# Causal linear attention in a fused Perceiver layer: the numerator matmuls go from 64x64 to 128x64 tiles, masking is done in two halves, and the Wo split moves from steps 2, 4, 6, 8 to steps 11 to 14

## The chip, the cores and the metric

The kernel runs on one core of a Trainium2 chip. The metric is device time of one launch in microseconds (us). The engines are called PE (TensorE, matmul), PEld (its weight loads), DVE (VectorE), ACT (ScalarE), POOL (GpSimd) and SP (SyncE, which here only issues DMAs). They run in parallel, each through its own list of instructions, and meet through semaphores.

## The reference, cut to what matters

```python
x = x + cross_attention(layernorm(x), ctx, ctx, Wq, bq, Wk, bk, Wv, bv)   # x (32, 32, 256), ctx (32, 257, 256)
x = x + linear_attention(layernorm(x), Wq, Wk, Wv, Wo, W_feat)
x = x + ffn(layernorm(x), w1, w2)     # two layers, 256 -> 1024 -> 256, ternary weights, 8-bit activations, gelu between

# linear_attention: H = 16 heads of 64, 128 features; T = 32 tokens in each of 32 sequences
q, k, v = heads(x @ Wq), heads(x @ Wk), heads(x @ Wv)
phi(u)  = exp(u @ W_feat - 0.5 * sum(u * u)) / sqrt(128)
num_t   = phi(q_t) @ sum_{s<=t} outer(phi(k_s), v_s)
den_t   = phi(q_t) @ sum_{s<=t} phi(k_s) + 1e-6
y = concat_heads(num / den) @ Wo
```

## The kernel before

The 1024 tokens lie in NG = 8 groups of 128 tokens (4 sequences each). The first stage is the cross attention. It goes over the groups and ends, for the matmul engine, at about 88 us. The third stage, the output projection with Wo and the feed-forward net, goes over the groups again and takes the time from about 214 us to the end. Between them stands the loop that the change touches.

**The head loop.** It has STEPS = 16 steps s. Step s treats two heads (`pair = s // 2`, inner index a) on one half of the tokens (`h = s % 2`, four groups g of 128 tokens). Each step has these parts:

- `project(s)`: q and k of the pair, 12 matmuls of 128x128 weights on 512 columns (L991 to L993, in split precision hi and lo).
- `squares(s)` on ACT and `copies(s)` on DVE take them out of PSUM; `squares_low(s)` on POOL makes the low part of the squares (`sq_lo`, L373).
- `exponents(s, t)`: 10 matmuls with weights of 64 rows and 128 columns (L1195); `features(s)` on ACT takes the exponential (`phi`, L563).
- `attention(s)`: scores phi(k) phi(q), in blocks of PT = 64 tokens (two sequences): 32 matmuls of tile 128x64 (all 128 rows of the array, 64 of its columns), L1208. A block b of 64 keys goes to partitions 64b to 64b + 63 of PSUM bank `b45[:, h]`.
- `masked(s)` on DVE: the scores times the causal mask, into SBUF tile `smk[h]` (L861).
- `numerators(s)`: the masked scores as weights, the values `va` (64 columns and a column of ones, which gives the denominator) as the moving side: 32 matmuls on 65 columns (L1220), into PSUM `b67`. Then `outputs(s)` on DVE divides (L871, L873, L876) and writes `y`.

PE's order is written by hand: in loop index i it does `project(i)`, `exponents(i-1, 0)`, `attention(i-2)`, `numerators(i-3)`, `exponents(i-1, 1)`. For i = 3 to 15 the numerators stand right behind the attention. After the loop come `exponents(15, 0)`, `attention(14)`, `numerators(13)`, `exponents(15, 1)`, `numerators(14)`, `attention(15)`, two groups of transposes `yTt(0, .)` (L1252), `numerators(15)`, and then `yTt(1, 0)` and `project_out(0)`. On DVE the end of the loop is `masked(14)`, `outputs(13)`, `outputs(14)`, `masked(15)`, `yTc(0, 0)`, `yTc(0, 1)`, `outputs(15)`. `numerators(s)` waits for `masked(s)` and for `outputs(s-1)`; `yTt(0, .)` waits for `outputs(14)`.

**POOL's side work.** Between the squares POOL splits the weights of the next head pair (`split_pair`, L348 and L350, in odd steps up to 13; `project` of the next even step waits for it), quantises the weights of the net (`quantise_w`, L383 to L387, a piece in each even step from 4 and two at the end) and splits Wo (`split_wo`, L393 and L395, in steps 2, 4, 6, 8).

**Loads.** SP issues all large loads in a written order. W1, W2 and Wo follow one another after the last `av_cp` of the cross attention (L293 to L295), then the loop's weights of pair 1. ACT sums the absolute values of W1 in index 1 and of W2 in index 2 of its loop (`weight_sum`, L497).

Of the kernel before, what the change touches and what calls it, by code (L numbers as in the profile page):

```python
# [16 lines left out]
F32 = mybir.dt.float32  # L17
F32R = mybir.dt.float32r
# [5 lines left out]
P = 128  # L24
# [4 lines left out]
PT = 2 * T  # L29
# [17 lines left out]
def build(nc, x, ctx, ctxT, xWq, bq, xWk, bk, xWvT, bv, aWq, aWk, aWv, aWo, Wf, w1T, w2T,  # L47
          ident_d, mask_d, seq_d, out):
    with ExitStack() as stack:
        def sem(name):  # L50
            return stack.enter_context(nc.semaphore(name))
# [69 lines left out]
        sq_lo = [[z2.take(f"sq_lo{h}{t}", [P, TOK], F32R) for t in range(2)] for h in range(2)]  # L121
        sq = [[z2.take(f"sq{h}{t}", [P, TOK]) for t in range(2)] for h in range(2)]
        w1_raw = z2.take("w1_raw", [P, DC, HID])
        w2_raw = z2.take("w2_raw", [P, HC, D])
        smk = [z2.take(f"smk{h}", [P, 2 * HALF, PT]) for h in range(2)]
        z = Region(work_at)
# [14 lines left out]
        cl = z.take("cl", [P, NG, D])  # L141
        z.at = max(z.at, z2.at - 2 * size[F32] * 2 * HALF * PT)
        xn2 = [z.take(f"xn2_{i}", [P, D]) for i in range(2)]
        z.at = max(z.at, z2.at)
        xwv_hi = z.take("xwv_hi", [P, DC, D], F32R)
# [3 lines left out]
        avT_lo = z.take("avT_lo", [P, DC, P], F32R)  # L149
        wo_lo = Region(z2.at).take("wo_lo", [P, HC, D], F32R)  # L150
        z3 = Region(work_at)
# [74 lines left out]
        f_mm, f_exp = sem("f_mm"), sem("f_exp")  # L226
        s_mm, s_mask = sem("s_mm"), sem("s_mask")
        n_mm, n_den, n_rden, n_y = (sem(n) for n in ("n_mm", "n_den", "n_rden", "n_y"))
# [12 lines left out]
        def _(sp):  # L241
# [50 lines left out]
            sp.wait_ge(av_cp, NG)  # L292
            sp.dma_start(w1_raw[:], w1T.rearrange("(c p) n -> p c n", p=P)).then_inc(ld_w1, 16)  # L293
            sp.dma_start(w2_raw[:], w2T.rearrange("(c p) n -> p c n", p=P)).then_inc(ld_w2, 16)
            sp.dma_start(wo[:], aWo.rearrange("(c p) n -> p c n", p=P)).then_inc(ld_wo, 16)  # L295
            for p in range(1, PAIRS):
                sp.wait_ge(w_split, p * 4)
                load_pair(p)
# [9 lines left out]
        def _(pool):  # L308
# [80 lines left out]
            def split_wo(k):  # L389
                if k == 0:  # L390
                    pool.wait_ge(ld_wo, 16)
                at = slice(2 * k, 2 * k + 2)
                nc.gpsimd.tensor_copy(wo_hi[:, at], wo[:, at]).then_inc(wo_split, 1)  # L393
                pool.wait_ge(wo_split, 2 * k + 1)
                nc.gpsimd.tensor_tensor(wo_lo[:, at], wo[:, at], wo_hi[:, at].bitcast(F32),  # L395
                                        ALU.subtract).then_inc(wo_split, 1)

            for s in range(STEPS):
                if s % 2 == 1 and s // 2 + 1 < PAIRS:
                    split_pair(s // 2 + 1, 2 * s + 1)  # L400
                squares_low(s)
                if s in (2, 4, 6, 8):
                    split_wo(s // 2 - 1)
                if s % 2 == 0 and s >= 4:
                    quantise_w(s // 2 - 2)
# [36 lines left out]
        def _(act):  # L442
# [186 lines left out]
            yTc(0, 1)  # L629
            act.wait_ge(s_mask, STEPS)  # L630
            for i in range(NG + 1):
# [19 lines left out]
        def _(dve):  # L651
# [205 lines left out]
            def masked(s):  # L857
                dve.wait_ge(s_mm, s + 1)
                if s >= 2:
                    dve.wait_ge(n_mm, s - 1)  # L860
                nc.vector.tensor_tensor(  # L861
                    smk[s % 2][:], b45[:, s % 2, :].rearrange("p (g n) -> p g n", n=PT),
                    mask[:].rearrange("p (a n) -> p a n", a=1).broadcast_to([P, 2 * HALF, PT]),
                    ALU.mult).then_inc(s_mask, 1)

# [15 lines left out]
            for i in range(1, STEPS):  # L881
                copies(i)
                if i == 4:
                    weight_scales()
                if i >= 2:
                    masked(i - 2)
                if i >= 3:
                    outputs(i - 3)
# [99 lines left out]
        def _(pe):  # L988
# [210 lines left out]
            def attention(s):  # L1199
                h = s % 2  # L1200
                pe.wait_ge(f_exp, 4 * s + 4)
                if s >= 2:
                    pe.wait_ge(s_mask, s - 1)
                for a in range(2):
# [7 lines left out]
            def numerators(s):  # L1212
                h, pair = s % 2, s // 2
                pe.wait_ge(s_mask, s + 1)
                if s >= 1:
                    pe.wait_ge(n_y, 2 * s)
                for g in range(HALF):
                    for b, a in ((0, 0), (1, 1), (0, 1), (1, 0)):
                        keys = slice(PT * b, PT * (b + 1))
                        mm = pe.matmul(b67[keys, a, g * VW:(g + 1) * VW], smk[h][keys, a * HALF + g, :],  # L1220
                                       va[keys, HALF * h + g, pair * 2 + a, :], start=True, stop=True)
                mm.then_inc(n_mm, 1)
# [6 lines left out]
            for i in range(2, STEPS):  # L1229
# [4 lines left out]
                if i == 4:  # L1234
                    pe.wait_ge(w_sum, 2)
                    pe.wait_ge(s_mask, 2)
                    pe.matmul(b5[:, 508:510], ones[:], wsum[:, 0:2], start=True, stop=True).then_inc(w_bc, 1)
# [167 lines left out]
```

## Time and profile before

| | |
|---|---|
| median of 3 runs | 272.37 us (271.4 to 272.67) |
| the profiled execution | 272.51 us |
| its span, from the first to the last instruction | 270.4 us |
| PE busy | 252.8 us, 94% of the span |
| DVE, ACT, POOL busy | 166.4, 142.4, 134.2 us |
| mean granted TensorE clock | 0.987 of full |

The first 2.11 us of difference between time and span lie outside of the recorded instructions. A busy share says how long an engine had an instruction in flight, not that it was at its peak: records of matmuls overlap, and short pauses between the starts of two matmuls are hidden in them. So the starts of neighbouring matmuls tell more than the busy time.

### The profile page before, as it was taken

The numbers are of one execution on the slowest core, as the hardware profiler recorded it, in microseconds if no ns is written. First come the engines' busy times: TensorE is split into PE (matmuls) and PEld (weight loads), VectorE is DVE, ScalarE is ACT, GpSimd is POOL, SyncE is SP. The second block draws the span as 40 slices with busy tenths as digits, with TensorE's granted clock in tenths as the row PEclk, the third lists the DMA queues.
The fourth block names the chain that finished last, engine by engine and source line by source line (L and its number), as shares of the span: only waits on it lengthen the run. The fifth ranks groups of instructions, "written<-read, shape, count | busy, mean of one in ns | idle before, by whom it ended". The sixth has DMA issues, their size and how long they took to land.

```text
span 270.4 us, 6580 instructions
## 1 busy us (share of the span) xinstructions
PE 252.8 (94%) x2568; PEld 198.9 (74%) x2574; DVE 166.4 (62%) x424; ACT 142.4 (53%) x267; POOL 134.2 (50%) x163
## 2 busy tenths in 40 slices
PE   8878849999999999999999999999998989999975
PEld 7765628786677667777777777777776978898754
DVE  3476856766644354655566555556662669898975
ACT  0432252544435688655545565545553537877762
POOL 2331202133103478497987979495889023434430
PEclk9999977999999999999999999999999999999999
DMA  6999999991078011001010010100000000010001
GB/s 207 367 385 367 374 320 342 364 394 44 1 236 270 0 41 40 2 0 41 2 40 2 2 42 0 41 2 0 2 0 2 2 2 0 6 36 25 19 19 58
DMA packets 18541, 27.74 MB, mean 103 GB/s; under 512 B 1488, under 2 KB 11856, under 8 KB 18512
## 3 DMA queue, kind: packets, MB, share of 16 engines
q1 hardware_dynamic: 17072, 26.35, 28.5%
q10 hardware_dynamic: 1440, 0.99, 1.2%
q8 instruction: 20, 0.33, 0.5%
q14 instruction: 9, 0.07, 0.1%
HBM read 26.28 MB, written 1.05 MB: 101 GB/s over the span
## 4 chain that ended last, share of the span: by engine, by line
PE 77%; SPq 6%; DMA 6%; ACT 4%; DVE 3%; issue 3%; POOL 0%; ACTq 0%
PE b L1195 16%; PE b L991 13%; PE b L993 11%; PE b L992 11%; PE b L1220 6%; DMA wv_raw<-in_aWv 6%; PE b L1208 6%; PE b L1252 2%; SPq L273 2%; PE b L1299 2%; PE b L1340 2%; PE b L1084 2%; PE b L1063 1%; SPq L269 1%; SPq L175 1%
## 5 line engine op out<-in xcount | busy, mean ns | idle before, releaser
L563 ACT ACTIVATE phi<-b 128x512 f32<-128x512 f32 x64 | 34.8, 598 | 40.8 <-PE b L1195 40.8
L373 POOL TENSOR_TENSOR sq_lo<-sq,sq_hi 128x512 fp32r<-128x512 f32 x32 | 40.9, 1290 | 23.6 <-ACT sq_hi L506 23.0
L791 DVE CAST x_hi<-b 128x512 fp32r<-128x512 f32 x32 | 22.1, 691 | 48.7 <-ACT sq_hi L506 48.7
L325 POOL TENSOR_TENSOR lnr<-lnv,mh 128x1 f32<-128x1 f32 x16 | 8.8, 548 | 54.3 <-DVE lnv L675 54.3
L991 PE MATMUL b<-nT_lo,wp_hi 128*128 128x512 f32 x64 | 26.8, 418 | 0.0
L505 ACT ACTIVATE sq<-b 128x512 f32<-128x512 f32 x32 | 19.2, 601 | 11.8 <-PE b L993 11.8
L993 PE MATMUL b<-nT_hi,wp_hi 128*128 128x512 f32 x64 | 25.1, 393 | 0.0
L992 PE MATMUL b<-nT_hi,wp_lo 128*128 128x512 f32 x64 | 24.9, 389 | 0.0
L793 DVE TENSOR_TENSOR x_lo<-b,x_hi 128x512 fp32r<-128x512 f32 x32 | 22.1, 691 | 1.1
L1208 PEld LDWEIGHTS b<-phi,phi 128*64 128x64 f32 x512 | 16.2, 138 | 5.7 <-issue 5.5
L506 ACT ACTIVATE sq_hi<-b 128x512 fp32r<-128x512 f32 x32 | 19.1, 595 | 0.0
L991 PE MATMUL b<-wo_lo,yT_hi 128*128 128x256 f32 x64 | 18.7, 293 | 0.0
L1208 PE MATMUL b<-phi,phi 128*64 128x64 f32 x512 | 18.4, 225 | 0.0
L1220 PE MATMUL b<-va,smk 64*64 64x65 f32 x512 | 18.4, 221 | 0.0
L993 PE MATMUL b<-wo_hi,yT_hi 128*128 128x256 f32 x64 | 18.1, 282 | 0.0
L992 PE MATMUL b<-wo_hi,yT_lo 128*128 128x256 f32 x64 | 18.0, 280 | 0.0
L1195 PE MATMUL b<-x_hi,feat_hi 64*128 64x512 f32 x64 | 16.7, 492 | 1.0 <-ACT phi L563 1.0
L991 PEld LDWEIGHTS b<-nT_lo,wp_hi 128*128 128x128 f32 x64 | 12.0, 187 | 7.5 <-issue 5.1
L1220 PEld LDWEIGHTS b<-va,smk 64*64 64x64 f32 x512 | 16.2, 134 | 1.6 <-issue 0.6
L444 ACT ACTIVATE va<-b 128x512 f32<-128x512 f32 x16 | 9.6, 599 | 11.3 <-PE b L993 11.3
L680 DVE TENSOR_SCALAR xn<-res,lnm,lnr 128x256 f32<-128x256 f32 x24 | 9.8, 421 | 8.6 <-POOL lnr L325 7.3
L991 PE MATMUL b<-wv_lo,nT_hi 128*128 128x512 f32 x32 | 14.1, 442 | 0.1
(162 smaller groups left out, 646.6 us busy)
## 6 DMA issues: line engine op xcount, KB each, us to landing
cT<-in_ctxT SPq DMA_DIRECT2D x8, 1028.0 KB, 13.9
cn<-in_ctx SPq DMA_DIRECT2D x8, 1024.0 KB, 15.4
wv_raw<-in_aWv SPq DMA_DIRECT2D x1, 1024.0 KB, 15.7
wp_raw<-in_aWq SPq DMA_DIRECT2D x8, 128.0 KB, 2.2
wp_raw<-in_aWk SPq DMA_DIRECT2D x8, 128.0 KB, 2.3
w_raw<-in_w1T SPq DMA_DIRECT2D x1, 1024.0 KB, 5.1
w_raw<-in_w2T SPq DMA_DIRECT2D x1, 1024.0 KB, 7.7
wo<-in_aWo SPq DMA_DIRECT2D x1, 1024.0 KB, 11.3
```

The source lines that it names most:

```text
L373: nc.gpsimd.tensor_tensor(sq_lo[s % 2][t][:], sq[s % 2][t][:], sq_hi[s % 2][t][:].bitcast(F32), ALU.subtract).then_inc(sq_l, 1)
L505: nc.scalar.activation(sq[s % 2][t][:], proj_bank(s, t), ACT.Square).then_inc(sq_f, 1)
L506: nc.scalar.activation(sq_hi[s % 2][t][:], proj_bank(s, t), ACT.Square).then_inc(sq_h, 1)
L563: nc.scalar.activation(phi[s % 2][t][a][:], (b2, b3)[a][:], ACT.Exp).then_inc(f_exp, 1)
L791: nc.vector.tensor_copy(x_hi[s % 2][t][:], proj_bank(s, t)).then_inc(x_h, 1)
L793: nc.vector.tensor_tensor(x_lo[s % 2][t][:], proj_bank(s, t), x_hi[s % 2][t][:].bitcast(F32), ALU.subtract).then_inc(x_l, 1)
L991: pe.matmul(acc, l_hi, r_lo, start=first, stop=False)
L992: pe.matmul(acc, l_lo, r_hi, start=False, stop=False)
L993: return pe.matmul(acc, l_hi, r_hi, start=False, stop=last)
L1195: mm = pe.matmul((b2, b3)[a][:], w[rows, :], v[rows, :], start=(n == 0), stop=(n == 4))
L1208: mm = pe.matmul(b45[PT * b:PT * (b + 1), h, (a * HALF + g) * PT:(a * HALF + g + 1) * PT], phi[h][1][a][:, at], phi[h][0][a][:, at], start ...
L1220: mm = pe.matmul(b67[keys, a, g * VW:(g + 1) * VW], smk[h][keys, a * HALF + g, :], va[keys, HALF * h + g, pair * 2 + a, :], start=True, st ...
```

## The change

1. `numerators(s)` uses tiles of 128 rows and 64 columns. The weights of block b are all 128 partitions of `smk[h][:, a * HALF + g, b, :]`, in which the 64 rows that belong to the other block are zeros, and the moving side is all 128 partitions of `va`. The order of the 32 matmuls is now a, g, b.
2. `smk` has a dimension more (twice the size). `masked(s)` writes block b of keys into its own place with one instruction for each half of the partitions, two in all. The zeros are written once, by four memsets on DVE (`clear_scores`) behind `copies(1)`.
3. `split_wo` is done in steps 11 to 14, and waits until W1 is quantised, since `wo_lo` now lies over `w1_raw`.
4. The loads come in the order W2, Wo, W1, and W1 waits for the last transposes `nT` of the first stage (`nT_mm`), since `w1_raw` now lies over tiles of that stage.

```diff
+        w2_raw = z2.take("w2_raw", [P, HC, D])
+        smk = [z2.take(f"smk{h}", [P, 2 * HALF, P // PT, PT]) for h in range(2)]
+        wo_lo = Region(z2.at).take("wo_lo", [P, HC, D], F32R)
         w1_raw = z2.take("w1_raw", [P, DC, HID])
-        w2_raw = z2.take("w2_raw", [P, HC, D])
-        smk = [z2.take(f"smk{h}", [P, 2 * HALF, PT]) for h in range(2)]
...
             sp.wait_ge(av_cp, NG)
-            sp.dma_start(w1_raw[:], w1T.rearrange("(c p) n -> p c n", p=P)).then_inc(ld_w1, 16)
             sp.dma_start(w2_raw[:], w2T.rearrange("(c p) n -> p c n", p=P)).then_inc(ld_w2, 16)
             sp.dma_start(wo[:], aWo.rearrange("(c p) n -> p c n", p=P)).then_inc(ld_wo, 16)
+            sp.wait_ge(nT_mm, NG)
+            sp.dma_start(w1_raw[:], w1T.rearrange("(c p) n -> p c n", p=P)).then_inc(ld_w1, 16)
...
             def split_wo(k):
                 if k == 0:
                     pool.wait_ge(ld_wo, 16)
+                    pool.wait_ge(w_quant, 4)
...
-                if s in (2, 4, 6, 8):
-                    split_wo(s // 2 - 1)
+                if s in (11, 12, 13, 14):
+                    split_wo(s - 11)
...
-                nc.vector.tensor_tensor(
-                    smk[s % 2][:], b45[:, s % 2, :].rearrange("p (g n) -> p g n", n=PT),
-                    mask[:].rearrange("p (a n) -> p a n", a=1).broadcast_to([P, 2 * HALF, PT]),
-                    ALU.mult).then_inc(s_mask, 1)
+                for b in range(P // PT):
+                    keys = slice(PT * b, PT * (b + 1))
+                    nc.vector.tensor_tensor(
+                        smk[s % 2][keys, :, b, :], b45[keys, s % 2, :].rearrange("p (g n) -> p g n", n=PT),
+                        mask[keys].rearrange("p (a n) -> p a n", a=1).broadcast_to([PT, 2 * HALF, PT]),
+                        ALU.mult).then_inc(s_mask, 1)
+
+            def clear_scores():
+
+                dve.wait_ge(nT_h, NG)
+                for h in range(2):
+                    for b in range(P // PT):
+                        nc.vector.memset(smk[h][PT * b:PT * (b + 1), :, 1 - b, :], 0.0).then_inc(s_zero, 1)
...
             for i in range(1, STEPS):
                 copies(i)
+                if i == 1:
+                    clear_scores()
...
                 if s >= 2:
-                    pe.wait_ge(s_mask, s - 1)
+                    pe.wait_ge(s_mask, 2 * (s - 1))
...
             def numerators(s):
                 h, pair = s % 2, s // 2
-                pe.wait_ge(s_mask, s + 1)
+                pe.wait_ge(s_mask, 2 * s + 2)
+                if s == 0:
+                    pe.wait_ge(s_zero, 4)
                 if s >= 1:
                     pe.wait_ge(n_y, 2 * s)
-                for g in range(HALF):
-                    for b, a in ((0, 0), (1, 1), (0, 1), (1, 0)):
-                        keys = slice(PT * b, PT * (b + 1))
-                        mm = pe.matmul(b67[keys, a, g * VW:(g + 1) * VW], smk[h][keys, a * HALF + g, :],
-                                       va[keys, HALF * h + g, pair * 2 + a, :], start=True, stop=True)
+                for a in range(2):
+                    for g in range(HALF):
+                        for b in range(P // PT):
+                            mm = pe.matmul(b67[PT * b:PT * (b + 1), a, g * VW:(g + 1) * VW],
+                                           smk[h][:, a * HALF + g, b, :], va[:, HALF * h + g, pair * 2 + a, :],
+                                           start=True, stop=True)
                 mm.then_inc(n_mm, 1)
```

The rest of the diff doubles the counts that other engines wait for on `s_mask`, and moves the start of the first stage's late tiles in SBUF.

**DVE at the end of a step of the head loop.** This is the kernel before, from the last copies of the loop on, with the semaphores that each row waits for:

```order
253 L791 CAST x_hi_98<-b 128x512 [waits f_mm,sq_h]
254 L793 TENSOR_TENSOR x_lo_102<-b,x_hi_98 128x512 [waits x_h]
255 L861 TENSOR_TENSOR smk_119<-b,mask 128x512 [waits n_mm,s_mm]
256 L871 TENSOR_SCALAR den<-b 128x8 [waits n_mm]
257 L873 RECIPROCAL rden<-den 128x8 [waits n_den]
258 L876 TENSOR_TENSOR y<-b,rden 128x4x64 [waits n_rden]
```

The same place of the changed kernel:

```order
246 L792 CAST x_hi_98<-b 128x512 [waits f_mm,sq_h]
247 L794 TENSOR_TENSOR x_lo_102<-b,x_hi_98 128x512 [waits x_h]
248 L864 TENSOR_TENSOR smk_118<-b,mask 64x8x64 [waits n_mm,s_mm]
249 L864 TENSOR_TENSOR smk_118<-b,mask 64x8x64
250 L881 TENSOR_SCALAR den<-b 128x8 [waits n_mm]
251 L883 RECIPROCAL rden<-den 128x8 [waits n_den]
```

One row of 128 partitions has become two rows of 64 partitions, and the division stands behind both.

**POOL in steps 11 to 13.** Before, between the squares of step 11 and the split of pair 7:

```order
100 L373 TENSOR_TENSOR sq_lo_112<-sq_116,sq_hi_108 128x512 [waits f_mm,sq_h,sq_f]
101 L373 TENSOR_TENSOR sq_lo_109<-sq_113,sq_hi_105 128x512 [waits f_mm,sq_h,sq_f]
102 L373 TENSOR_TENSOR sq_lo_110<-sq_114,sq_hi_106 128x512 [waits f_mm,sq_h,sq_f]
103 L383 TENSOR_SCALAR w2q<-w_raw,wsum 128x512
104 L385 TENSOR_SCALAR w_raw<-w_raw,wsum 128x512 [waits w_low]
105 L387 TENSOR_TENSOR w2q<-w_raw,w2q 128x512 [waits w_low]
106 L348 CAST wp_hi<-wp_raw 128x256 [waits a_mm,ld_qk]
```

The changed kernel there:

```order
92 L373 TENSOR_TENSOR sq_lo_112<-sq_116,sq_hi_108 128x512 [waits f_mm,sq_h,sq_f]
93 L394 CAST wo_hi<-wo 128x512 [waits w_quant,ld_wo]
94 L396 TENSOR_TENSOR wo_lo<-wo,wo_hi 128x512 [waits wo_split]
95 L373 TENSOR_TENSOR sq_lo_109<-sq_113,sq_hi_105 128x512 [waits f_mm,sq_h,sq_f]
96 L373 TENSOR_TENSOR sq_lo_110<-sq_114,sq_hi_106 128x512 [waits f_mm,sq_h,sq_f]
97 L394 CAST wo_hi<-wo 128x512
98 L396 TENSOR_TENSOR wo_lo<-wo,wo_hi 128x512 [waits wo_split]
99 L383 TENSOR_SCALAR w2q<-w_raw,wsum 128x512
100 L385 TENSOR_SCALAR w_raw<-w_raw,wsum 128x512 [waits w_low]
101 L387 TENSOR_TENSOR w2q<-w_raw,w2q 128x512 [waits w_low]
102 L348 CAST wp_hi<-wp_raw 128x256 [waits a_mm,ld_qk]
```

Two pieces of the Wo split stand there now; steps 13 and 14 have one more each.

**SP behind the last loads of the context.** Before, W1, W2, Wo and the first weights of pair 1:

```order
29 L293 DMA w_raw<-in_w1T 128x2x1024 [waits av_cp]
30 L294 DMA w_raw<-in_w2T 128x8x256
31 L295 DMA wo<-in_aWo 128x8x256
32 L256 DMA wp_raw<-in_aWq 128x2x128 [waits w_split]
33 L256 DMA wp_raw<-in_aWk 128x2x128
```

In the changed kernel:

```order
29 L292 DMA w_raw<-in_w2T 128x8x256 [waits av_cp]
30 L293 DMA wo<-in_aWo 128x8x256
31 L295 DMA w_raw<-in_w1T 128x2x1024 [waits nT_mm]
32 L255 DMA wp_raw<-in_aWq 128x2x128 [waits w_split]
33 L255 DMA wp_raw<-in_aWk 128x2x128
```

W1 is third now and has a wait of its own, and the weights of pair 1 stand behind it.

## Rows read from the trace of the kernel before

**Rows 1.** Windows, the head loop: us, busy us of each engine, granted clock

```profile
104.05:205.50 101.45, 100.67 (x1249) 76.17 (x1248) 58.25 (x120) 56.12 (x104) 80.86 (x77) 1.00 0.05 15
```

**Rows 2.** The chain that ended last, in step 8: start us, us, what

```profile
144.76 1.08 PE b L1208 x32
145.84 1.08 PE b L1220 x32
```

**Rows 3.** Timeline, PE where the numerators follow the attention: start us, us, what

```profile
145.38 0.46 PE L1208 MATMUL b<-phi,phi 128*64 128x64 f32 x9
145.77 0.33 PE L1220 MATMUL b<-va,smk 64*64 64x65 f32 x4
```

**Rows 4.** The page's costliest groups: busy us, mean ns of one

```profile
L1208 PE MATMUL b<-phi,phi 128*64 128x64 f32 x512 | 18.4, 225 | 0.0
L1220 PE MATMUL b<-va,smk 64*64 64x65 f32 x512 | 18.4, 221 | 0.0
```

**Rows 5.** Timeline, PE in the first stage, two kinds of one tile size

```profile
46.90 1.07 PE L1084 MATMUL b<-cn,pT 128*32 128x256 f32 x16
...
47.35 0.61 PE L1084 MATMUL b<-cn,pT 128*32 128x256 f32 x8
47.78 0.39 PE L1063 MATMUL b<-cT,qkT 128*32 128x257 f32 x3
```

**Rows 6.** Timeline, DVE in steps 8 and 9; in brackets the idle time before

```profile
143.18 0.69 DVE L791 CAST x_hi<-b 128x512 fp32r<-128x512 f32 x1 [2.84 <-ACT sq_hi L506]
...
145.89 0.69 DVE L861 TENSOR_TENSOR smk<-b,mask 128x512 f32<-128x512 f32 x1
146.97 0.17 DVE L871 TENSOR_SCALAR den<-b 128x8 f32<-128x8 f32 x1 [0.39 <-PE b L1220]
...
151.00 0.69 DVE L791 CAST x_hi<-b 128x512 fp32r<-128x512 f32 x1 [2.84 <-ACT sq_hi L506]
```

**Rows 7.** Timeline, DVE behind `copies(1)`

```profile
97.80 0.69 DVE L791 CAST x_hi<-b 128x512 fp32r<-128x512 f32 x1 [2.81 <-ACT sq_hi L506]
```

**Rows 8.** Timeline, PE and DVE at the end of the head loop

```profile
206.79 0.69 DVE L861 TENSOR_TENSOR smk<-b,mask 128x512 f32<-128x512 f32 x1 [3.85 <-PE b L1208]
207.87 0.17 DVE L871 TENSOR_SCALAR den<-b 128x8 f32<-128x8 f32 x1 [0.39 <-PE b L1220]
...
208.31 0.76 DVE L876 TENSOR_TENSOR y<-b,rden 128x256 f32<-128x256 f32 x2
...
209.21 1.15 PE L1220 MATMUL b<-va,smk 64*64 64x65 f32 x32
...
211.55 0.69 DVE L861 TENSOR_TENSOR smk<-b,mask 128x512 f32<-128x512 f32 x1
211.65 1.09 PE L1252 MATMUL b<-ident,y 128*128 128x128 f32 x8
212.67 0.28 PE L1220 MATMUL b<-va,smk 64*64 64x65 f32 x2
```

**Rows 9.** Timeline, POOL from the squares of step 8 to those of step 9

```profile
143.28 2.67 POOL L373 TENSOR_TENSOR sq_lo<-sq,sq_hi 128x512 fp32r<-128x512 f32 x2 [1.79 <-ACT sq_hi L506]
145.88 0.61 POOL L393 CAST wo_hi<-wo 128x512 fp32r<-128x512 f32 x1
...
147.83 1.57 POOL L383 TENSOR_SCALAR w1q<-w_raw,wsum 128x512 bf16<-128x512 f32 x1
...
152.27 0.39 POOL L348 CAST wp_hi<-wp_raw 128x256 fp32r<-128x256 f32 x1
...
154.59 2.54 POOL L373 TENSOR_TENSOR sq_lo<-sq,sq_hi 128x512 fp32r<-128x512 f32 x2
```

**Rows 10.** Timeline, SP's issue of the Wo load, and who uses loads

```profile
76.17 0.58 SPq L295 DMA_DIRECT2D wo<-in_aWo  x1
...
91.20 0.40 POOL L348 CAST wp_hi<-wp_raw 128x256 fp32r<-128x256 f32 x1 [4.71 <-PE b L993]
...
94.79 1.91 ACT L497 ACTIVATE w1q<-w_raw 128x2048 bf16<-128x2048 f32 x1
```

**Rows 11.** The page's DMA issues: KB each, us to landing

```profile
wo<-in_aWo SPq DMA_DIRECT2D x1, 1024.0 KB, 11.3
```

More of the change, by code:

```diff
@@ L141, in build @@
         cl = z.take("cl", [P, NG, D])
-        z.at = max(z.at, z2.at - 2 * size[F32] * 2 * HALF * PT)
+        z.at = max(z.at, z2.at - 2 * size[F32] * 2 * HALF * P - size[F32] * DC * HID)
         xn2 = [z.take(f"xn2_{i}", [P, D]) for i in range(2)]
-        z.at = max(z.at, z2.at)
         xwv_hi = z.take("xwv_hi", [P, DC, D], F32R)
@@ L149, in build @@
         avT_lo = z.take("avT_lo", [P, DC, P], F32R)
-        wo_lo = Region(z2.at).take("wo_lo", [P, HC, D], F32R)
         z3 = Region(work_at)
@@ L226, in build @@
         f_mm, f_exp = sem("f_mm"), sem("f_exp")
-        s_mm, s_mask = sem("s_mm"), sem("s_mask")
+        s_mm, s_mask, s_zero = sem("s_mm"), sem("s_mask"), sem("s_zero")
         n_mm, n_den, n_rden, n_y = (sem(n) for n in ("n_mm", "n_den", "n_rden", "n_y"))
@@ L629, in _ @@
             yTc(0, 1)
-            act.wait_ge(s_mask, STEPS)
+            act.wait_ge(s_mask, 2 * STEPS)
             for i in range(NG + 1):
@@ L1235, in _ @@
                     pe.wait_ge(w_sum, 2)
-                    pe.wait_ge(s_mask, 2)
+                    pe.wait_ge(s_mask, 4)
                     pe.matmul(b5[:, 508:510], ones[:], wsum[:, 0:2], start=True, stop=True).then_inc(w_bc, 1)
```

## The prediction

> **What bounds the kernel now.** I read the busy shares first, then the windows of the head loop, then the chain that ended last, and then the timeline of single matmuls. In the loop's window PE is busy for 100.67 of 101.45 us and the granted clock is 1.00, while DVE has 58.25, ACT 56.12 and POOL 80.86 us of work [rows 1]. The chain confirms it: within a step it runs through PE alone, the attention for 1.08 us and the numerators for 1.08 us [rows 2]. So a nanosecond less on PE in the loop is one less in the time, as long as no other engine becomes late, and work on DVE or POOL costs nothing while it fits into their gaps.
>
> The two blocks of 32 small matmuls have the same length, though one has tiles of 128 rows and one of 64. They come in pairs, one for each half of the array's columns. Nine attention matmuls take 0.46 us with the duration of the last [rows 3], which is 0.225 us [rows 4]; the starts of these four further pairs are thus (0.46 - 0.225) / 4 = 0.059 us apart. The last of them starts at 145.38 + 0.235 = 145.615, and the first of the numerators at 145.77 [rows 3]. That is 0.155 us instead of 0.059, a pause of 0.096. The next pair is late too: four numerator matmuls take 0.33 us, less 0.22 for the last one, which puts the second pair 0.11 behind the first, 0.05 more than the steady 0.059 [rows 3, 4]. Together the passage costs 0.15 us. The length of the block says the same: 1.08 - 16 x 0.059 = 0.14 [rows 2].
>
> **What the passage is made of.** Either the array pauses because the tile size changes from 128x64 to 64x64, or because the first weight load waits for semaphores, though these have long been given. The first stage tells them apart: L1063 follows L1084 with the same tile 128x32 and with semaphore waits of its own. Two groups of four L1084 take 47.35 - 46.90 = 0.45 us, and the next two, up to the first start of L1063, 47.78 - 47.35 = 0.43 us [rows 5]. There is no pause there. So I put the 0.15 us to the change of the tile size.
>
> The Trainium skill, "TensorEngine Tiling (Array Packing)", Key Properties, says that a change of the tiling mode, not of the tile alone, drains TensorE; the row of L1063 agrees, as there the mode stays and nothing is lost.
>
> **The change, part by part.**
>
> *Numerators in 128x64 tiles.* The number of matmuls (32) and their columns (65) stay. The nearest row for the new shape is the attention's own: 128x64, 64 columns, 0.059 us for a pair [rows 3]. The old tile with 65 columns does 0.059 too, so the column more costs nothing. The block stays at 0.94 us of steady pairs, and the passage from the attention to it loses its pause: -0.15 us at each place where numerators follow attention. These are i = 3 to 15, 13 places, and attention(14) with numerators(13), the 14th. The passage from the numerators to the exponents remains a change of tile size (to 64x128) and I keep its price. The first 13 carry on into PE's own chain: 13 x 0.15 = 1.95 us. The 14th does not, as DVE takes over there (below).
>
> *Masking in halves.* A half has 64 partitions but the same 512 elements in each. I price it as the whole one, 0.69 us, with starts 0.68 us apart, the mean of the four instructions from 143.18 to 145.89 [rows 6]; the other end is half of it, if partitions counted. In the steady loop the division now starts behind both halves, at about 145.89 + 1.3 = 147.2 instead of 146.97, and there is 2.84 us of idle time behind it before the next step's copies [rows 6]. Queued behind the second half are only these: the division, whose result the next numerators want a whole step later, and the copies. Cost 0.
>
> At the end of the loop it is not hidden. masked(14) starts at 206.79, and outputs(13) started at 207.87 when numerators(13) ended [rows 8]. With two halves outputs(13) starts at 206.79 + 1.3 = 208.1, 0.2 us later, relative to the attention before it. numerators(14) waited for the end of this division (208.31 + 0.76 = 209.07, start of the matmuls 209.21 [rows 8]), so it shifts by 0.2, and with it outputs(14), the transposes at 211.65 and masked(15) at 211.55. The latter now ends at 211.55 + 0.2 + 0.65 + 0.69 = 213.1. numerators(15) started at 212.67, right when PE had done the transposes [rows 8]; it now waits for the mask until about 213.15. That is 0.5 us later, and PE goes on from it to the output projection. Cost of the end: +0.5 us. If a half cost half, it would be 0; at 0.8 us for a half it would be 0.8.
>
> *Clearing.* Four memsets of 64x512 behind copies(1). DVE is idle for 2.81 us there [rows 7]; at the pace of its 512-element instructions they take 4 x 0.68 = 2.7 us and end just inside. Cost 0; if they took 1 us each, 1.2 us of delay for the copies of step 2, in a stretch where ACT is late as well.
>
> *Wo split later.* From the starts in step 8: two squares 2.60, a piece of Wo 1.95, a piece of quantising 4.44, a pair split 2.32 us [rows 9]. A step is 151.00 - 143.18 = 7.82 us [rows 6], and will be 7.67. Step 11 has 2.32 + 2.60 + 1.95 = 6.87, step 12 8.99, step 13 6.87, step 14 8.99. Step 10 leaves POOL behind its input by no more than step 8 did (there the squares started on their input after an idle 1.79), and step 11 ends about 1.4 us before the squares of step 12 can start. Step 12 is then exactly step 8 of before: squares, Wo, quantising, and the pair split at +8.99 us. In step 8 that was in time: the chain has no POOL in it [rows 2]. The cycle is 0.15 us shorter, no more. Step 14 starts 0.5 us late, step 15 some 1.8, and sq_lo is wanted a step later. Cost 0.
>
> *Loads.* Wo was issued at 76.17 and landed 11.3 us later, with W1 and W2 ahead of it, so 3 MB had come by 87.5 [rows 10, 11]. Now W1 goes out after the last nT, at about 81, when W2 and half of Wo have come; it is the last of the same 3 MB, so it lands at 87 to 89. ACT wants it at 94.79 [rows 10]. The weights of pair 1 stand behind it, some 1 us more, and POOL wants them at 91.20 [rows 10]. Cost 0, with 2 us of cover for the nearer one.
>
> **Sum.** -1.95 + 0.5 = -1.45 us. The profiled execution had 270.4 us of span and 2.11 us around it; 268.95 + 2.11 = 271.06, and since that execution lies 0.14 above the median of the runs, the new median is 270.9 us, -0.5%. About 0.5% is also what a measurement of this kernel can tell from no change.
>
> **Rivals.**
>
> *The pause stays.* If the wait on the mask, and not the tile size, holds back the weight load, nothing is won at the 13 places and the end costs its 0.5: 272.9 us. Against it stand [rows 5]; for it, that these are other instructions, in pairs of two and not four.
>
> *The new tiles don't run side by side.* Old pairs differed in rows and columns of the array, new pairs share all rows. If they went one after another, each would take half of a transposing matmul of 128 columns; eight of those take 1.09 us up to the next block, which starts at 212.67 after 211.65, 0.127 apart [rows 8]. That makes 0.064 a matmul, 2.0 us a block instead of 0.94, 16 times: +17 us less the 1.45, about 288 us. The break-even lies where a pair costs 0.065 instead of 0.059 (1.45 us over 256 pairs). Against it: the attention has this very shape and does 0.059.
>
> The Trainium skill, "TensorE: Matmul & The Clock Gate", Part 3, says that weight loads overlap with matmuls in flight only when the row group differs, which speaks against this change: by it the new pairs would be slower than the old ones, toward that 288 us. The attention's pairs share their rows and are as fast as the old numerators, so the rows here don't bear it out.
>
> *Something is late in its place.* The split of pair 7 after step 12, the loads of W1 and pair 1, or the memsets. If the loads took the 2 us of cover and 2 us more, ACT, then the copies, then PE would be late by these: 270.9 + 2 = 272.9 us. POOL decides when a step 12 takes over 1 us longer than step 8 did.
>
> *More is won.* The halves are cheap and the end costs nothing, and the 14th place counts: 14 x 0.15 = 2.1 us, 270.3 us.
>
> **How the numbers follow.** Forecast 0.62 (270.5 to 271.4, from 0.3 to 0.8 for the end and the spread of the runs), the pause stays 0.17, not side by side 0.05, something late 0.08, more won 0.08. The range reaches from the last, less the runs' spread, 270.0, to the pause that stays, 272.9. The forecast lies on the border of 0.5% (271.0): 0.4 of its 0.62 goes to faster, 0.22 to no change. With the other cases: faster 0.47, same 0.43, slower 0.10.
>
> **What would show it.** In the changed profile the starts of the numerators should follow the last attention pair by 0.06 us and not 0.15, the chain's piece for both blocks together should be 2.01 instead of 2.16 us, and the step 7.67. The mask's rows should come in two of about 0.69 us with 64 partitions. At the end numerators(15) should wait for DVE's mask. W1 should land by 89 us, and no POOL wait should stand ahead of project(14). The prediction is wrong if the pause is still there, if a new block takes over 1.08 us, or if PE waits within steps 3 to 15.

## The result, and the profile after

The changed kernel takes 271.19 us (median of 22 runs) where the kernel before takes 272.52 beside it. The ratio is 0.9939, with a 95% interval of 0.9917 to 0.996: faster by 0.6%. Ratios and intervals, here and below, are taken over the executions that were not in the slow state (over 1.5% above a kernel's fastest), so they are not just the quotients of the medians. The profiled execution has a span of 269.3 us.

PE's place of interest first. These are two groups of the page of the changed kernel (busy us, mean ns of one), and then its timeline where the numerators follow the attention (start us, us, what; in brackets the idle time before).

```profile
L1234 PE MATMUL b<-va,smk 128*64 128x65 f32 x512 | 17.8, 222 | 0.8 <-DVE y L886 0.5
L1220 PE MATMUL b<-phi,phi 128*64 128x64 f32 x512 | 18.4, 225 | 0.0
```

```profile
144.32 0.46 PE L1220 MATMUL b<-phi,phi 128*64 128x64 f32 x10
144.62 0.35 PE L1234 MATMUL b<-va,smk 128*64 128x65 f32 x6
```

The first row holds ten attention matmuls; (0.46 - 0.225) us lie between the first and the last start, so the last one starts at 144.555. The numerators follow at 144.62, 0.06 us later, where it was 0.155 [rows 3]. Six of them, three pairs, take 0.35 us, less 0.222 for the last: 0.13 us for two gaps, 0.06 each, where the first gap alone was 0.11. Both parts of the pause are gone. The chain that ended last says it in whole blocks:

```profile
143.70 1.08 PE b L1220 x32
144.79 0.94 PE b L1234 x32
145.72 1.36 PE b L1207 x10
...
151.38 1.08 PE b L1220 x32
```

The numerators' piece is 0.94 instead of 1.08 [rows 2], and the step, from one attention to the next, 7.67 instead of 7.82 us.

DVE has more to do. In the window of the head loop it is busy for 66.88 us, where it was 58.25 in the window of before [rows 1], and PE is still the full engine (the first column behind the comma is PE's, the third DVE's):

```profile
103.74:203.35 99.61, 98.83 (x1251) 75.22 (x1250) 66.88 (x133) 56.21 (x105) 81.09 (x77) 1.00 0.05 15
```

Its timeline within a step shows the two halves of the mask, the division behind them, and the next step's copies:

```profile
144.84 1.41 DVE L864 TENSOR_TENSOR smk<-b,mask 64x512 f32<-64x512 f32 x2
146.27 0.17 DVE L881 TENSOR_SCALAR den<-b 128x8 f32<-128x8 f32 x1
...
149.81 0.69 DVE L792 CAST x_hi<-b 128x512 fp32r<-128x512 f32 x1 [2.35 <-ACT sq_hi L507]
```

The division no longer waits for PE, as it did for 0.39 us in [rows 6]; the mask hides that. The idle time ahead of the copies has shrunk from 2.84 to 2.35 us and still covers all. At the end of the loop it does not. This is the timeline there, PE and DVE:

```profile
204.52 1.41 DVE L864 TENSOR_TENSOR smk<-b,mask 64x512 f32<-64x512 f32 x2 [3.34 <-PE b L1220]
205.96 0.17 DVE L881 TENSOR_SCALAR den<-b 128x8 f32<-128x8 f32 x1
...
207.30 1.15 PE L1234 MATMUL b<-va,smk 128*64 128x65 f32 x32 [0.53 <-DVE y L886]
...
209.60 1.40 DVE L864 TENSOR_TENSOR smk<-b,mask 64x512 f32<-64x512 f32 x2
...
209.74 1.09 PE L1267 MATMUL b<-ident,y 128*128 128x128 f32 x8 [0.35 <-DVE y L886]
...
211.06 1.15 PE L1234 MATMUL b<-va,smk 128*64 128x65 f32 x32 [0.23 <-DVE smk L864]
```

Three waits of PE on DVE are marked, 0.53, 0.35 and 0.23 us, where [rows 8] have none. The middle one is not new, it has grown: before, attention(15) ended at 210.35 + 1.15 = 211.50 us and the transposes started at 211.65 [rows 8], a wait of 0.15 us, which the timeline does not mark.

```profile
210.35 1.15 PE L1208 MATMUL b<-phi,phi 128*64 128x64 f32 x32
```

From the first matmul of attention(14) to the first of the output projection it takes 9.23 us; before, 8.60.

So the two profiles differ thus: from attention(1) to attention(14) 98.20 us instead of 100.15, that is -1.96; to the output projection +0.63; in sum -1.33. The first stage came out 0.31 us shorter in this execution, which no edit explains. Up to attention(1) the twelve profiles of this study differ by 2.6 us (104.0 to 106.6), and much of that goes with the granted clock. The shortest and one of the two longest, in their first 100 us (the third number from the end is the mean of the granted clock, which is at its full level of 2.4 GHz there but for a stretch at half of it):

```profile
0.00:100.00 100.00, 89.64 (x703) 68.67 (x704) 59.73 (x178) 43.37 (x93) 28.32 (x43) 0.98 0.72 251
0.00:100.00 100.00, 88.96 (x692) 68.52 (x692) 58.11 (x175) 42.38 (x92) 27.56 (x43) 0.95 0.73 251
```

At 0.98 attention(1) started at 104.0, 104.4 and 104.8 us, at 0.97 at 105.1 to 106.6 (seven profiles, the kernel before and the changed one among them), at 0.95 at 106.2 and 106.6. The whole times follow the clock too: of 85 executions of the kernel before that ran beside the experiments, the 36 with a mean clock of 0.992 or more took 272.0 us on average, the 39 with 0.984 to 0.987 took 272.9 and the 10 with 0.981 or less took 274.3. So much of what makes the times of one kernel differ is the clock. And at the very end something stands that I had not looked at. The chain of the changed kernel and, below it, that of the kernel before:

```profile
263.95 2.57 DMA out<-fin
...
266.64 0.48 DVE fin L972
```

```profile
265.94 1.76 PE b L1340 x16
...
267.73 0.48 DVE fin L960
```

The last group's result goes into the buffer of group 5 and waits until that has been stored. In the profile of before, PE was the last to arrive; in that of the changed kernel it was the store, and this costs 0.56 us (final(7) starts 1.43 us behind final(6) instead of 0.87). That is why the spans differ by 1.1 us only.

What holds the store up can be seen in the DMA view. For each kernel this is the window from just before the issue of that store to 1.8 us later, before and then changed (packets, MB, share of 16 engines; then the store's KB and its time to landing):

```profile
q1 hardware_dynamic: 144, 0.13, 21.4%
out<-fin SPq DMA_DIRECT2D x1, 128.0 KB, 1.7
```

```profile
q1 hardware_dynamic: 138, 0.13, 21.6%
q8 instruction: 1, 0.02, 4.1%
out<-fin SPq DMA_DIRECT2D x1, 128.0 KB, 2.6
```

In the changed kernel a 16 KB load of instructions runs at the same time. Of the store's 144 packets 135 start as before, and the last nine, a sixteenth, only from the end of that load on (to within 0.02 us); three of these nine fall into the window. The store lands 1.14 us after the load's end. In the kernel before, such a load comes 5.7 us later, behind all stores.

### The profile page after: what moved, and what is told of

It is laid out like the page before. It is cut to its first block, busy times and chain, and to the rows that moved or that the text cites. A ratio compares the mean times of both kernels' runs of the same rounds, so it can differ in the third digit from the quotient of the medians.

```text
span 269.3 us, 6602 instructions
## 1 busy us (share of the span) xinstructions
PE 250.3 (93%) x2568; PEld 197.5 (73%) x2574; DVE 178.5 (66%) x444; ACT 142.3 (53%) x267; POOL 133.9 (50%) x163
## 4 chain that ended last, share of the span: by engine, by line
PE 74%; DMA 7%; SPq 6%; DVE 4%; ACT 4%; issue 3%; POOL 0%; ACTq 0%; DVEq 0%
PE b L1207 16%; PE b L1003 13%; PE b L1005 11%; PE b L1004 11%; DMA wv_raw<-in_aWv 6%; PE b L1220 6%; PE b L1234 5%; SPq L272 2%; PE b L1314 2%; PE b L1267 2%; PE b L1096 2%; PE b L1355 1%; PE b L1075 1%; SPq L268 1%; SPq L174 1%
## 5 line engine op out<-in xcount | busy, mean ns | idle before, releaser
L864 DVE TENSOR_TENSOR smk<-b,mask 64x512 f32<-64x512 f32 x32 | 22.0, 687 | 3.8 <-PE b L1220 3.3
L1234 PE MATMUL b<-va,smk 128*64 128x65 f32 x512 | 17.8, 222 | 0.8 <-DVE y L886 0.5
L1234 PEld LDWEIGHTS b<-va,smk 128*64 128x64 f32 x512 | 16.3, 138 | 1.4 <-issue 0.9
```

What stands on the lines that cost most here:

```text
L864: nc.vector.tensor_tensor(smk[s % 2][keys, :, b, :], b45[keys, s % 2, :].rearrange("p (g n) -> p g n", n=PT), mask[keys].rearrange("p (a n ...
L1234: mm = pe.matmul(b67[PT * b:PT * (b + 1), a, g * VW:(g + 1) * VW], smk[h][:, a * HALF + g, b, :], va[:, HALF * h + g, pair * 2 + a, :], st ...
```

## The experiments

All times are medians, and the ratios are against the kernel before on the same chip. The rows below the second were measured on three chips, on which the kernel before had 272.94 us (old tiles to moves only, and the first whole mask in 14 and 15), 272.18 us (whole mask in step 15, halves by columns, Wo split in step 12, own buffer) and 272.82 us (the last two rows). "Step" is the median distance from one attention to the next, and "tail" the time from the first matmul of attention(14) to the first of the output projection, both in the profiled execution. They hardly vary: two executions of a same kernel gave 9.227 and 9.224 us of tail.

| kernel | step, us | tail, us | time, us | ratio | 95% interval |
|---|---|---|---|---|---|
| before | 7.826 | 8.601 | 272.52 | | |
| the change | 7.673 | 9.227 | 271.19 | 0.9939 | 0.9917 to 0.996 |
| old tiles | 7.826 | 9.225 | 273.53 | 1.0032 | 1.0005 to 1.006 |
| halves only | 7.826 | 9.220 | 273.3 | 1.0012 | 0.9987 to 1.0036 |
| moves only | 7.826 | 8.599 | 273.68 | 1.0009 | 0.998 to 1.0039 |
| whole mask in steps 14, 15 | 7.673 | 8.455 | 270.59 | 0.9904 | 0.9875 to 0.9933 |
| whole mask in step 15 | 7.673 | 8.958 | 271.33 | 0.9951 | 0.992 to 0.9982 |
| halves by columns | 7.827 | 8.605 | 272.84 | 0.9999 | 0.9971 to 1.0028 |
| Wo split in step 12 | 7.673, once 9.414 | 9.229 | 273.68 | 1.004 | 1.0013 to 1.0066 |
| last result in its own buffer | 7.673 | 8.449 | 270.69 | 0.9933 | 0.9901 to 0.9966 |
| the change again | 7.673 | 9.224 | 271.09 | 0.9954 | 0.9925 to 0.9982 |
| whole mask in 14, 15 again | 7.673 | 8.454 | 271.15 | 0.9952 | 0.9918 to 0.9986 |

**Old tiles.** One edit to the changed kernel:

```diff
-                for a in range(2):
-                    for g in range(HALF):
-                        for b in range(P // PT):
-                            mm = pe.matmul(b67[PT * b:PT * (b + 1), a, g * VW:(g + 1) * VW],
-                                           smk[h][:, a * HALF + g, b, :], va[:, HALF * h + g, pair * 2 + a, :],
+                for g in range(HALF):
+                    for b, a in ((0, 0), (1, 1), (0, 1), (1, 0)):
+                        keys = slice(PT * b, PT * (b + 1))
+                        mm = pe.matmul(b67[keys, a, g * VW:(g + 1) * VW], smk[h][keys, a * HALF + g, b, :],
+                                       va[keys, HALF * h + g, pair * 2 + a, :], start=True, stop=True)
```

> The changed kernel with one edit: the numerators go back to 64x64 tiles in their old order, reading the two blocks of the doubled smk; masking in halves, memsets, Wo split and loads stay changed. Theory (the tile size makes the pause): behind the attention the first numerators again start 0.155 us after the last attention pair and the second pair 0.11 after the first, a step is 7.82 us again, the loop's gain of 1.95 us is gone and the tail's cost of 0.6 us stays, so 273.1 us where before has 272.5 (ratio 1.002). Rival (the gain came from somewhere else in the change, such as the order of matmuls, the buffers or the loads): the step stays at 7.67 us and the ratio at 0.994.

The step is 7.826 us again, and the time is over that of before. The chain has the old piece back:

```profile
145.16 1.08 PE b L1220 x32
146.24 1.08 PE b L1234 x32
```

The waits ahead of the numerators are those of the changed kernel, and only the tiles differ. So the pause comes and goes with the numerators' tiles, and the whole gain is this pause. The order of the 32 matmuls went back too, and the order alone was not tried. The first matmul is the same in both orders, and 0.096 of the 0.15 us lie ahead of it; of the 0.05 behind it, the order as a cause is not excluded.

**Halves only.** The kernel before, with the mask in two instructions into the old `smk`:

```diff
+                for b in range(P // PT):
+                    keys = slice(PT * b, PT * (b + 1))
+                    nc.vector.tensor_tensor(
+                        smk[s % 2][keys], b45[keys, s % 2, :].rearrange("p (g n) -> p g n", n=PT),
+                        mask[keys].rearrange("p (a n) -> p a n", a=1).broadcast_to([PT, 2 * HALF, PT]),
+                        ALU.mult).then_inc(s_mask, 1)
```

> The kernel before with one edit: masking in two instructions of 64 partitions into the old smk. Theory: a half takes 0.69 us like the whole, nothing changes in the steady steps (7.82 us), and from attention(14) to the first matmul of the output projection it takes 9.2 instead of 8.6 us; 273.1 us, ratio 1.002. Rival (half the partitions, half the time): 0.35 us each, no difference at the end, ratio 1.000. Rival (DVE becomes late in the steady steps): the step is longer than 7.82 us and the loss is over 2 us.

The steady steps don't feel it, and the tail is 9.22 us: all of the loss at the end of the loop belongs to the halves. The ratio, 1.0012, lies between the theory's 1.002 and 1.000, and its interval holds both, so the size is shown by the trace and not by the times.

**Moves only.** The kernel before, with the Wo split and the loads in their new order:

```diff
-                if s in (2, 4, 6, 8):
-                    split_wo(s // 2 - 1)
+                if s in (11, 12, 13, 14):
+                    split_wo(s - 11)
...
+            sp.wait_ge(nT_mm, NG)
+            sp.dma_start(w1_raw[:], w1T.rearrange("(c p) n -> p c n", p=P)).then_inc(ld_w1, 16)
```

> The kernel before with the Wo split in steps 11 to 14 behind the fourth quantised piece, and W1 loaded last behind the last nT, with the old places of the tiles. Theory: both are under cover, the step is 7.82 us from 3 to 15 and the ratio 1.000. Rival (POOL is late for the pair split after step 12, or W1 or pair 1 is late): a wait of PE on POOL ahead of project(14), or of ACT on the W1 load, and a ratio of 1.003 or more.

Step and tail are those of before to 2 ns. PE has one marked wait from 104 us to the end of the loop, on ACT, and the kernel before has it too:

```profile
PE b L1197 <- ACT phi L565: 0.8, 1, 0.8
```

**Wo split in step 12.** How much cover the moved work has was measured by using it up:

```diff
-                if s in (11, 12, 13, 14):
-                    split_wo(s - 11)
+                if s == 12:
+                    split_wo(0)
+                    split_wo(1)
+                    split_wo(2)
+                if s == 14:
+                    split_wo(3)
```

> The changed kernel with three of the four pieces of the Wo split in step 12 (the fourth in 14) instead of one in each of steps 11 to 14: 3.9 us more of POOL work ahead of the split of pair 7. Theory (POOL's side work is free only up to some 2.3 us more than step 12 has): wp_lo of pair 7 is ready 3.9 us later than its 183.1 in the changed kernel, so about 187.0, project(14) starts there instead of at 185.4, PE waits 1.6 us for POOL at this one place, and the time is 1.6 us over the changed kernel's, ratio about 1.000. Rival (this work is under cover wherever it stands): no wait, ratio 0.994.

One step is 9.41 us long, 1.74 more than its neighbours; 1.6 was expected. The timeline shows whom PE waits for:

```profile
186.16 0.40 POOL L348 CAST wp_hi<-wp_raw 128x256 fp32r<-128x256 f32 x1
...
186.35 0.47 PE L1007 MATMUL b<-nT_lo,wp_hi 128*128 128x512 f32 x1 [1.68 <-POOL wp_lo L350]
```

So in the changed kernel the split of pair 7 has about 3.9 - 1.7 = 2.2 us of cover. The same POOL work, put badly, takes the whole gain: in the trace, attention(1) to attention(14) is 0.21 us shorter than before and the tail 0.63 longer, +0.4 us. The measured ratio is further off, 1.004 where 1.000 was expected, or 1.1 us, and its interval lies wholly above 1. Part of this may be the clock, which was 0.986 on average in these executions and 0.990 in those of the kernel before beside them; the rest is open.

**Whole mask in steps 14 and 15.** In the changed kernel, the last two steps go back to one instruction and to 64x64 tiles, since they are where DVE's time counts and PE's pause does not:

```diff
+                if s >= WHOLE:
+                    nc.vector.tensor_tensor(
+                        smk[s % 2][:, :, 0, :], b45[:, s % 2, :].rearrange("p (g n) -> p g n", n=PT),
+                        mask[:].rearrange("p (a n) -> p a n", a=1).broadcast_to([P, 2 * HALF, PT]),
+                        ALU.mult).then_inc(s_mask, 1)
+                    return
```

> The changed kernel, but steps 14 and 15 are masked by one instruction over 128 partitions into the first block of smk, and their numerators use the 64x64 tiles of before. Theory (the tail's 0.6 us is the second half of the mask twice on the path): the steady steps keep 7.67 us, and from attention(14) to the output projection it takes 8.6 us as before, 8.45 at best; 270.5 us where before has 272.5, ratio 0.9925, against 0.9939 for the changed kernel. Rival (the tail's loss has another cause, such as the tile size at its four passages): 9.2 us stay and the ratio is 0.994.

The tail is 8.455 us, 0.77 less than in the changed kernel and 0.15 less than before; the steps stay at 7.673. The timeline marks none of the three waits on DVE any more (the transposes start 0.13 us behind attention(15), as they did 0.15 before):

```profile
204.94 0.69 DVE L870 TENSOR_TENSOR smk<-b,mask 128x512 f32<-128x512 f32 x1 [3.34 <-PE b L1233]
...
207.22 1.15 PE L1248 MATMUL b<-va,smk 64*64 64x65 f32 x32
...
209.57 0.69 DVE L870 TENSOR_TENSOR smk<-b,mask 128x512 f32<-128x512 f32 x1
...
210.68 1.15 PE L1248 MATMUL b<-va,smk 64*64 64x65 f32 x32
```

**Whole mask in step 15 alone** (WHOLE = 15 in the same code):

> The changed kernel with step 15 alone masked in one piece and with 64x64 tiles. Theory (the tail's loss has two parts, the second half of masked(14) on the way to numerators(14), and that of masked(15) on the way to numerators(15)): numerators(14) stay 0.36 us late, numerators(15) are late by that alone, so from attention(14) to the output projection 8.9 to 9.0 us, between 8.46 and 9.23; ratio 0.993. Rival (the mask of step 15 alone costs it): 8.5 us; rival (that of step 14 alone): 9.2 us.

8.96 us: of the 0.77, 0.27 belong to the mask of step 15 and 0.50 to that of step 14. The second is the larger because it also takes what the 14th missing pause gives: numerators(14) start 3.62 us behind attention(14) in the kernel before, 3.98 in the changed one and 3.48 with both masks whole, 0.15 earlier than before.

**Halves by columns.** The kernel before, with the mask in two instructions of all partitions and half of the columns:

```diff
+                for a in range(2):
+                    nc.vector.tensor_tensor(
+                        smk[s % 2][:, HALF * a:HALF * (a + 1), :],
+                        b45[:, s % 2, HALF * PT * a:HALF * PT * (a + 1)].rearrange("p (g n) -> p g n", n=PT),
```

> The kernel before with masking in two instructions of all 128 partitions and 256 elements each, instead of one of 512. Theory (a DVE instruction costs its elements in one partition, and an instruction on fewer partitions saves nothing): 0.42 us for one and starts 0.34 apart, as the two instructions of y, so both together 0.07 to 0.1 us over the whole one; from attention(14) to the output projection 8.6 to 8.7 us and a ratio of 1.000. Rival (each more instruction costs some 0.7 us whatever its size): 9.2 us and 1.002.

```profile
206.67 0.76 DVE L862 TENSOR_TENSOR smk<-b,mask 128x256 f32<-128x256 f32 x2 [3.85 <-PE b L1210]
```

Both together take 0.76 us, where two halves by partitions take 1.41 and the whole 0.69. The tail is that of before. It is the elements in a partition that cost, not the number of instructions.

**The last result in its own buffer**, on top of the whole mask in steps 14 and 15:

```diff
+        fin_last = z3.take("fin_last", [P, D])
...
-                if g >= 2:
+                if 2 <= g < LAST:
                     dve.wait_ge(stored[g % 2], 16 * (g // 2))
```

> The version that masks steps 14 and 15 in one piece, with one more edit: the last group's result has a buffer of its own, so final(7) does not wait for the store of group 5. Theory (this store's landing, which differs from run to run, ends last in part of the executions): final(7) starts 0.87 us behind final(6) as in the profile of before, not 1.4 to 2.1 as in four other profiles, and the time falls by 0.3 to 1 us against the version without it: ratio 0.987 to 0.9915. Rival (the final wait for all stores at the end takes the same time anyway, so it only changes places): ratio stays at 0.990 to 0.9925.

The wait is gone from the chain, and final(7) starts 0.874 us behind final(6):

```profile
264.97 1.76 PE b L1377 x16
...
266.75 0.48 DVE fin_last L986
```

In the other eleven profiles this distance was 0.87 us three times and 1.43 to 2.42 eight times, and the traces tell what sets the two kinds apart. The three are the kernel before, moves only and halves by columns: their store landed in 1.7 us, with no load of instructions beside it. The eight are all those that mask by halves of the partitions in some step: there the 16 KB load fell on the store, which landed in 2.57 to 3.54 us, always 1.1 to 1.2 us after the load's end. The version with its own buffer has the same (2.96 us), but nobody waits for it. Why the load comes some 5 us earlier in these nine is open, and so is whether it does in every execution of these kernels, as no kernel has more than two profiles. The number of instructions on DVE doesn't settle it: halves by columns and halves only have the same, 560 recorded in each, and are of different kinds.

But the times show no gain: 0.9933 here and 0.9904 and 0.9952 without the edit, with intervals that overlap. 0.9933 lies above what theory (to 0.9915) and rival (to 0.9925) expected. Whether the buffer is worth something stays open.

**The ranking.** The changed kernel and the version with the whole mask in the last two steps were run again, side by side.

> The changed kernel as it is, beside the next one on the same chip, to set the two against each other. Expected: steps of 7.67 us and 9.23 us from attention(14) to the output projection, ratio 0.994 to before.

> The version that masks steps 14 and 15 in one piece, beside the changed kernel on the same chip. Theory (the trace's 9.23 - 8.46 = 0.77 us at the end is time): 0.8 us, or 0.3%, below the changed kernel, ratio 0.991 to before. Rival (given back later, in the stage behind, at the store that the last group waits for): the same time as the changed kernel, ratio 0.994.

The tails repeat to 3 ns, 9.224 and 8.454 us, but the times are the same, 271.09 and 271.15 us. In the two pairs of runs the version was once better by 0.35% (against the changed kernel's own first measurement) and once not at all. 0.77 us is 0.28%, and each of these intervals is some 0.3% wide on either side. So the trace shows the tail shorter by 0.77 us, and the times can't tell whether the kernel is. The rival isn't refuted. From the output projection to final(6) all profiles take 52.62 to 52.72 us, so nothing is given back there. At the store that the rival names, final(7) starts 1.43 and 2.28 us behind final(6) in the two profiles of the changed kernel and 1.78 and 1.59 in the two of this version: no sign of giving back, but the spread is as large as the 0.77 us.

## Why the prediction was right, step by step

**What bounds the loop: right.** PE's starts set the step in all of the profiles, and what was taken from PE came off the time.

**The pause, 0.15 us: right in cause and size.** The step went from 7.826 to 7.673 us, 0.153, and the 13 places gave 1.96 us where the sum had 1.95. Old tiles with all else changed brought it back. The rival that the pause stays, at 0.17, and that of tiles that don't run side by side, at 0.05, both fall by the changed kernel's timeline: pairs of 128x64 start 0.06 us apart. How much of this belongs to the order of the matmuls was not tried.

The Trainium skill, "TensorE: Matmul & The Clock Gate", Part 3, has weight loads overlap only when the row group differs; the changed kernel's pairs share all rows and their whole block takes 0.94 us, no slower a pair than the old ones, so here the measurement decides against it. The Trainium skill's "TensorEngine Tiling (Array Packing)", Key Properties, has the drain at a change of mode, and the trace agrees: the passage from 128x64 to 64x64 cost 0.15 us, and with one mode on both sides the cost is gone.

**The masks in halves at the end, +0.5: the term that was mis-sized.** It measured 0.63. The prediction priced two halves at 0.68 between starts and let outputs(13) start 0.2 us later. They started 0.72 us apart and the division another 0.72 behind (204.52, 205.96), so it was 1.44 instead of 1.08 us after the mask's begin, and numerators(14) came 0.36 us late. Of the price for a half, 0.69 like the whole, 0.688 was measured.

**The clearing, cost 0: right.** The memsets took 0.48 us each and started 0.65 apart, less than the 0.68 that was assumed, and DVE was still idle for 0.32 us behind them.

**Wo split and loads, cost 0: right.** Moves only changed nothing. W1 was issued at 80.87 us and landed 6.4 us later, at 87.3, within the 87 to 89 of the prediction. The cover ahead of project(14) is 2.2 us, by the run that used it up.

**The sum.** -1.96 + 0.63 = -1.33 us, by the parts. The forecast had -1.45. The measured ratio makes -1.7 us, with an interval of -1.1 to -2.3, so both lie in it. Of the 0.3 us by which the median, 271.19, lies over the forecast of 270.9, 0.15 is the kernel before, which had 272.52 instead of 272.37 in the longer series, and 0.12 the parts.

What no step of the prediction had is the wait for the store of group 5. It cost 0.56 and 1.41 us in the two profiles of the changed kernel and nothing in the one of before. With it, and without the first stage, the profiles differ by about -0.8 and 0.0 us, which the interval of -1.1 to -2.3 does not hold. So either other executions of the kernel before wait for the store too, or something gives it back; only one execution of it was profiled, so this is open. That the forecast of the whole came out so close is in this part luck: it left out a term as large as the one for the end of the loop.

## What to carry to other kernels

Where a full TensorE goes through blocks of small matmuls, look at the starts of matmuls at the border between two blocks: a change of tile size cost 0.15 us there and showed in no busy share, and padding with zeros to the neighbour's tile size cost nothing on that engine, since the time of such a matmul did not depend on its rows. What the padding costs elsewhere (here an instruction more on DVE in each step) is free inside the loop and not at its end, so treat the last steps by themselves. After an edit, look at the DMA view around the last stores as well: a load of instructions may have moved onto them. Side work may be moved only as far as the next instruction that someone waits for on the same engine; the way to know the cover is to use it up once.

## What was not expected of the hardware

- Two DVE instructions on different halves of the partitions don't overlap: starts 0.71 us apart at 0.69 each, and the next instruction 0.73 behind. Two whole ones behind one another with no wait between start 0.61 apart, and two on 256 columns 0.34 at 0.42 each. The two halves thus cost more than twice the spacing of a whole one.
- A 16 KB load of instructions can hold up a store. The store of group 5, 128 KB in 144 packets, landed in 1.7 us in three profiles without such a load beside it and in 2.57 to 3.54 us in nine with one. In these nine its last nine packets started when the load ended, to within 0.02 us.
- The granted clock in the first stage differs from execution to execution of one kernel (0.95 to 0.98 over the first 100 us), and the time differs with it, by 2.3 us between the groups named in the section on the result.
